# Two durations in a build-time instruction planner set to other values: the issue and the landing of the loads of split rows

## The chip, the core and the metric

The kernel runs on one core of a Trainium2 chip. The metric is the device time of one launch in microseconds (us); each kernel is run several times and the median is compared. Times of single instructions come from one profiled execution.

## What is computed

Two transformer layers over 4 batches of 1024 tokens with 256 features, 16 heads of 16. Cut to what matters, with layer normalisation after each residual sum:

```python
x = norm(x + L0_attn(x))   # rotary, causal softmax within a window of 64 tokens
x = norm(x + L0_ffn(x))    # token shift, sigmoid gate, squared relu
x = norm(x + L1_attn(x))   # linear attention over random features
x = norm(x + L1_ffn(x))    # a whole block: norm, rotary, full causal softmax, then a routed
                           # feed-forward: 8 experts, top 2, capacity 1024 each
```

All of it is float32 at the inputs and outputs.

## The kernel before

There are two stages. The **first stage** holds both attentions, the two small feed-forward and linear-attention parts, and the routing. The **second stage** runs the 8 experts and the last normalisation. The second stage is written in a fixed order and the change doesn't reach it.

The first stage is cut into 32 groups of 4 heads, in this order: 4 windowed groups of batch 0, 4 windowed of batch 1, 4 full of batch 0, 4 windowed of batch 2, 4 full of batch 1, and so on; so groups 0 to 3 are windowed, 8 to 11 full, 20 to 23 windowed. Two groups make a pair, and each pair is prepared together (`prep`): projections (`proj`, L928), rotary products, sums on GpSimd (`add`), transposes back (`turn`, L947), and a split of each float32 row into three bfloat16 parts (`high`, `mid`, `low`) in the tile `b_split`. Twelve **loads** per group (`load`, L760, issued by SyncE, 128 KB each) bring the parts into one of three ring tiles `b_qk`. A group's `max` products (a mask product L955 or L958, then L962) wait for all twelve of its loads. Their row maxima are reduced on VectorE (`reduce`, L1378), turned (`rows`, L968), written back to `b_qk` by a small DMA (`spread`, L767), and then the `exp` products (L975), the exponentials on ScalarE (L1114) and the products with the values (`values`, L989) follow; `out` (L997) turns the sums back.

No engine's order is written by hand. The class `Planner` lists every step with an engine, an assumed cost and what it comes after, and simulates the engines at build time. At each moment an idle engine takes, among the steps that are ready by the plan, the one with the longest chain of assumed costs behind it. A step that follows one on another engine becomes ready after that engine's delay in `LATE`, or, if it follows a DMA, after that kind's entry in `LANDING`. What comes out is a program for each engine, which the hardware then runs in that order with semaphores. SyncE's order is planned in the same way: the loads, the spreads, and the `zeros` (L790), 32 DMAs of 256 KB that clear a DRAM buffer, are all in one queue.

The plan leaves one more mark in the program. Where it sees TensorE idle for more than 1.0 us before a step that takes a PSUM bank, filler products (L808) are put in front of that step, for 0.6 of the planned idle time at 0.064 us each:

```python
for n in range(int(FILLED * plan.idle[x] / FILLER) if plan.idle[x] > LEAST_IDLE else 0):
    pe.matmul(u.psum[:, plan.bank[x], 0:P], u.id16[:, :], u.id16[:, :], start=True, stop=True, ...
```

The names that the prediction uses: `LANDING` in `Planner`, `load` inside `describe` of `Plan`, the pair's last `turn` (L947), a group's first `max` (L955 or L958), the fillers (L808), the `zeros` (L790) and the spreads (L767).

## Time and profile before

| | us |
|---|---|
| median of 3 runs (lowest to highest) | 1862.9 (1861.72 to 1863.72) |
| the profiled execution | 1861.47 |
| its span, first to last instruction | 1859.7 |
| TensorE busy | 1733.4 (93%) |
| VectorE busy | 1016.1 (55%) |
| ScalarE busy | 886.3 (48%) |
| GpSimd busy | 835.7 (45%) |
| mean granted TensorE clock, share of full speed | 0.975 |

In the profile PE is TensorE, PEld its weight loads, DVE VectorE, ACT ScalarE, POOL GpSimd and SPq the DMA queue of SyncE. A row names the source line, the operation and the tiles it writes and reads. Busy time doesn't count waiting for semaphores. The granted clock is the share of TensorE's full speed (2.4 GHz) that it was given.

### The profile page before, as it was taken

Reading aid. Unit: us, or ns where it says so; the run is one execution under the profiler, and the core shown is the slowest. Engines: PE = TensorE matmul, PEld = TensorE weight load, DVE = VectorE, ACT = ScalarE, POOL = GpSimd, SP = SyncE. Lnnn points to the kernel's source line nnn. Section 1 sums busy time; section 2 is a strip of 40 time slices with the busy share of each in tenths; the row PEclk is TensorE's granted clock in tenths of the full one; section 3 lists DMA queues with packets and bytes.
Section 4 is the critical chain, followed back from the end, with each engine's and each line's share of the span. In section 5 each row is a group of like instructions: output and inputs, shape, how many; then the busy total and the mean of one; then the engine's idle time right before and its main releaser. Section 6 shows DMA issues by size and latency. Waiting matters only on the chain. (4 is left out here: it accounts for less than half of the span.)

```text
span 1859.7 us, 34083 instructions
## 1 busy us (share of the span) xinstructions
PE 1733.4 (93%) x11399; PEld 1130.5 (61%) x11399; DVE 1016.1 (55%) x2357; ACT 886.3 (48%) x1877; POOL 835.7 (45%) x1295
## 2 busy tenths in 40 slices
PE   6899998999999899999999999999879999999992
PEld 5666765665476656557765654544647766667771
DVE  4557677868567985857698677885401100011014
ACT  2455463657756365675637467566322222212223
POOL 4674663522368683137868323455432211221223
PEclk9999999999999999999999999999889999999996
DMA  6725337132343313234512214242033233332116
GB/s 211 95 71 68 44 103 131 19 52 92 47 71 75 87 24 47 70 50 69 91 29 36 35 47 70 44 76 71 29 122 85 40 65 83 90 88 62 20 23 192
DMA packets 106055, 131.27 MB, mean 71 GB/s; under 512 B 15882, under 2 KB 77467, under 8 KB 105744
## 3 DMA queue, kind: packets, MB, share of 16 engines
q1 hardware_dynamic: 89488, 117.08, 29.6%
q0 software_dynamic: 14336, 11.41, 4.5%
q8 instruction: 98, 1.61, 0.4%
q14 instruction: 69, 0.57, 0.2%
q10 hardware_dynamic: 2064, 0.61, 0.2%
HBM read 53.96 MB, written 38.01 MB: 49 GB/s over the span
## 5 line engine op out<-in xcount | busy, mean ns | idle before, releaser
L1114 ACT ACTIVATE b_probs<-b_psum 128x512 f32<-128x512 f32 (+3 forms) x896 | 417.8, 546 | 184.3 <-PE b_psum L975 182.6
L1378 DVE TENSOR_REDUCE b_mneg<-b_psum 128x2 f32<-128x384 f32 (+5 forms) x608 | 331.9, 591 | 88.5 <-PE b_psum L962 87.2
L1477 POOL TENSOR_SCALAR_AFFINE_SELECT b_probs<-b_probs 128x512 f32<-128x512 f32 (+1 forms) x400 | 239.3, 610 | 284.7 <-ACT b_probs L1114 273.9
L962 PE MATMUL b_psum<-b_qk 96*128 96x192 bf16 (+4 forms) x1280 | 292.5, 294 | 3.1 <-DVE b_mhalf L1378 1.1
L975 PE MATMUL b_psum<-b_qk 99*128 99x192 bf16 (+5 forms) x1344 | 261.5, 289 | 11.3 <-DMA b_qk<-b_mrow 7.0
L1711 POOL DMA_INDIRECT before_last_norm<-b_ye,b_ids x64 | 99.1, 1549 | 347.6 <-DMA before_last_norm<-b_ye,b_ids 195.2
L1808 ACT ACTIVATE b_hid<-b_psum,b_b 128x512 f32<-128x512 f32 (+1 forms) x136 | 90.0, 662 | 336.1 <-PE b_psum L1751 336.1
L1852 DVE TENSOR_TENSOR b_ye<-b_psum,b_qk 128x512 f32<-128x512 f32 (+1 forms) x33 | 22.3, 675 | 388.5 <-PE b_psum L1759 388.5
L989 PE MATMUL b_psum<-b_probs,b_v 128*32 128x192 f32 (+4 forms) x2688 | 197.6, 414 | 3.8 <-POOL b_probs L1477 3.0
L962 PEld LDWEIGHTS b_psum<-b_qk 96*128 96x128 bf16 x1280 | 122.8, 99 | 93.4 <-issue 24.7
L1378 DVE TENSOR_REDUCE b_mhalf<-b_psum 128x1 f32<-128x512 f32 x256 | 165.0, 680 | 15.0 <-PE b_psum L962 14.3
L975 PEld LDWEIGHTS b_psum<-b_qk 99*128 99x128 bf16 x1344 | 113.3, 98 | 91.5 <-issue 22.7
L1493 POOL TENSOR_TENSOR b_rot<-b_product 128x128 f32<-128x128 f32 x256 | 113.1, 474 | 120.3 <-PE b_psum L947 52.5
L989 PEld LDWEIGHTS b_psum<-b_probs,b_v 128*32 128x32 f32 x2688 | 68.6, 109 | 92.7 <-issue 66.5
L1361 DVE TENSOR_TENSOR b_product<-b_psum,b_cossin 128x512 f32<-128x512 f32 x128 | 87.7, 687 | 56.5 <-PE b_psum L928 50.6
L928 PE MATMUL b_psum<-b_wqkv,b_xt 128*128 128x384 f32 x320 | 116.7, 493 | 0.5 <-ACT b_xt L1020 0.3
L1759 PE MATMUL b_psum<-b_w,b_hid 128*128 128x256 f32 x512 | 111.6, 379 | 0.6 <-ACT b_hid L1808 0.6
L1751 PE MATMUL b_psum<-b_xgt,b_qk 128*128 128x512 f32 x256 | 110.9, 593 | 0.4 <-ACT b_xgt L1798 0.4
L1759 PE MATMUL b_psum<-b_qk,b_hid 128*128 128x256 f32 x512 | 111.2, 379 | 0.0
L1751 PE MATMUL b_psum<-b_xgt,b_w 128*128 128x512 f32 (+1 forms) x288 | 110.9, 545 | 0.0
L1759 PEld LDWEIGHTS b_psum<-b_w,b_hid 128*128 128x128 f32 x512 | 97.0, 190 | 14.0 <-ACT b_hid L1808 1.0
L1759 PEld LDWEIGHTS b_psum<-b_qk,b_hid 128*128 128x128 f32 x512 | 97.0, 190 | 13.0
(227 smaller groups left out, 2772.9 us busy)
## 6 DMA issues: line engine op xcount, KB each, us to landing
b_qk<-b_split SPq DMA_DIRECT2D x372, 128.0 KB, 5.5
slot_rows<-before_last_norm SPq DMA_DIRECT2D x32, 256.0 KB, 3.9
b_qk<-in_W SPq DMA_DIRECT2D x8, 1024.0 KB, 7.5
b_xg<-slot_rows SPq DMA_DIRECT2D x16, 512.0 KB, 9.6
b_w<-in_W SPq DMA_DIRECT2D x8, 1024.0 KB
before_last_norm<-b_early SPq DMA_DIRECT2D x4, 1024.0 KB, 4.4
b_o<-before_last_norm SPq DMA_DIRECT2D x4, 1024.0 KB, 5.5
before_last_norm<-b_o SPq DMA_DIRECT2D x4, 1024.0 KB, 4.5
```

What stands on the lines that cost most here:

```text
L928: ins = pe.matmul(u.psum[:, plan.bank[x], 0:384].rearrange("p (a g y) -> p a g y", a=3, g=2), x_rows[:, c, P * t:P * t + P], (u.wqkv0 if n ...
L962: ins = pe.matmul(out[:, i, :], q[0:KS, h, P * t:P * t + P], q[0:KS, HG + h, a:e], start=not last, stop=True, skip_group_check=True)
L975: ins = pe.matmul(out[:, i, :], q[0:KM, HG + h, P * t:P * t + P], q[0:KM, h, a:e], start=True, stop=True, skip_group_check=True)
L989: ins = pe.matmul(sums_of(g, h2)[32 * h:32 * h + 32, a - BANK * h2:e - BANK * h2], u.v[:, g % 4, t, (HD + 1) * h:(HD + 1) * h + 32], probs ...
L1114: act.activation(probs_of((g, h2, t), a, e)[:, heads[0]:heads[-1] + 1, :], bank, ACT.Exp, scale=SCALE).then_inc(s.exp_done, 1)
L1378: dve.tensor_reduce(out, in_bank(("max",) + x[1:], heads, e - a), AX.X, ALU.max, negate=True).then_inc(s.max_read, 1)
L1477: ins = pool.affine_select(out=block, in_=block, pattern=[[0, HG], [1 if ahead else -1, z - y]], compare_op=ALU.is_ge, fill=none, base=y - ...
L1493: ins = pool.tensor_tensor(out[:, :, :, HALF * y:HALF * y + HALF], straight[:, :, :, HALF * y:HALF * y + HALF], crossed[:, :, :, HALF * (1 ...
L1711: pool.indirect_dma_start(out=x4_dram, out_offset=bass.IndirectOffsetOnAxis(ap=u.ids[:, column:column + 1], axis=0), in_=u.ye[t // 2][:, t ...
L1751: ins = pe.matmul(u.psum[:, k % 4, 0:hi - lo], u.w1[e % 2][:, c, P * n:P * n + P], u.xgt[:, c, lo:hi], start=(c == 0), stop=(c == NC - 1))
L1759: ins = pe.matmul(u.psum[:, bank_of(e, t), D * (t % 2):D * (t % 2) + D], u.hid[:, n, P * t:P * (t + 1)], u.w2[e % 2][:, n, :], start=(n == ...
L1808: act.activation(u.hid[:, n, lo:hi], u.psum[:, k % 4, 0:hi - lo], ACT.Gelu, bias=u.b1[:, NF * e + n:NF * e + n + 1]).then_inc(s.h_done, 1)
```

## The change

Two assumed durations of the loads of split rows are replaced. The time from issue to landing becomes 5.1 in place of 4.5, and the time that SyncE takes for one issue becomes 0.69 in place of 1.05. Only the loads of group 0 keep their own issue cost of 0.55.

```diff
-    LANDING = {"load": 4.5, "spread": 2.2, "source": 4.0, "x3_in": 3.0, "x3_out": 3.0, "x4_out": 3.0, "put": 2.5, "zeros": 6.0, "expert": 8.0}
+    LANDING = {"load": 5.1, "spread": 2.2, "source": 4.0, "x3_in": 3.0, "x3_out": 3.0, "x4_out": 3.0, "put": 2.5, "zeros": 6.0, "expert": 8.0}
...
-                        add(("load", g, a, slot, y), "SP", 0.55 if y is not None else 1.05, (kind, g // 2, q), last)
+                        add(("load", g, a, slot, y), "SP", 0.55 if y is not None else 0.69, (kind, g // 2, q), last)
```

No instruction of the computation is added or removed. The program of each engine is another order of the same steps, and the number of fillers is another: 475 in 26 places before, 348 in 15 places now. The last three places (50, 12 and 22 fillers) are the same in both. Up to the first filler place and in the last 131 rows of TensorE the two orders agree; between, they differ nearly throughout. Three places are shown.

TensorE near the start, after the second half of group 0's `max` products, as one piece of the difference (- before, + now). L808 are the fillers, L968 turns the row maxima of group 0, L928 are the projections of the second pair:

```order
 L955 MATMUL b_psum<-b_mask_q,b_id 128x2x192
 L962 MATMUL b_psum<-b_qk 128x192 x2
-L808 MATMUL b_psum<-b_id 128x128 x32
-L968 MATMUL b_psum<-b_id,b_mparts 128x128 x4
+L808 MATMUL b_psum<-b_id 128x128 x14
 L928 MATMUL b_psum<-b_wqkv,b_xa 128x384 x8
 L947 MATMUL b_psum<-b_id,b_rot 128x128 x4
```

The projections now come ahead of the turn of the maxima, with 18 fillers fewer before them.

TensorE up to the first `max` of group 20, whose first row is L955. The pair's last `turn` is the row L947. Before, that row stands 13 rows above the first one shown, and behind the rows shown come twelve short L975 (128x384, 128x256 and 128x128, four each) and L955:

```order
L997 MATMUL b_psum<-b_id,b_ot_sb 128x128 x4
L989 MATMUL b_psum<-b_probs,b_v 32x256 x4
L989 MATMUL b_psum<-b_probs,b_v 32x128 x4
L975 MATMUL b_psum<-b_qk 128x512 x8
L997 MATMUL b_psum<-b_id,b_ot_sb 128x128 x8
L808 MATMUL b_psum<-b_id 128x128 x12
L722 MATMUL b_psum<-b_id,b_y 128x128 x8
L989 MATMUL b_psum<-b_probs,b_v 32x512 x8
L975 MATMUL b_psum<-b_qk 128x512 x12
L716 MATMUL b_psum<-b_wproj,b_early 128x256 x4
L989 MATMUL b_psum<-b_probs,b_v 32x512 x8
```

Now, from the last `turn` on; behind the rows shown come one more L997 x4, L989 512 x8, the same twelve short L975, and L955:

```order
L947 MATMUL b_psum<-b_id,b_rot 128x128 x4
L975 MATMUL b_psum<-b_qk 128x512 x5
L989 MATMUL b_psum<-b_probs,b_v 32x256 x4
L989 MATMUL b_psum<-b_probs,b_v 32x128 x4
L997 MATMUL b_psum<-b_id,b_ot_sb 128x128 x4
L975 MATMUL b_psum<-b_qk 128x512
L997 MATMUL b_psum<-b_id,b_ot_sb 128x128 x4
L722 MATMUL b_psum<-b_id,b_y 128x128 x4
L997 MATMUL b_psum<-b_id,b_ot_sb 128x128 x4
L989 MATMUL b_psum<-b_probs,b_v 32x512 x8
L975 MATMUL b_psum<-b_qk 128x512 x12
```

The pair's last `turn` has moved nearer to the first `max` that needs its loads, and the fillers and the projection L716 have gone from between them.

SyncE's queue around the loads of groups 8 and 9; L760 are the loads, L790 the zeros, L767 the spreads. Before:

```order
L767 DMA b_qk<-b_mrow 3x4x512
L760 DMA b_qk<-b_split 16x4x1024 x10
L790 DMA slot_rows<-before_last_norm 128x2x256 x7
L760 DMA b_qk<-b_split 16x4x1024
L767 DMA b_qk<-b_mrow 3x4x512
L760 DMA b_qk<-b_split 16x4x1024 x13
```

Now:

```order
L760 DMA b_qk<-b_split 16x4x1024 x4
L767 DMA b_qk<-b_mrow 3x4x512
L760 DMA b_qk<-b_split 16x4x1024 x2
L790 DMA slot_rows<-before_last_norm 128x2x256 x2
L760 DMA b_qk<-b_split 16x4x1024 x4
L790 DMA slot_rows<-before_last_norm 128x2x256 x4
L760 DMA b_qk<-b_split 16x4x1024 x12
```

Group 8's twelve loads now have six zeros and one spread between them, where they had seven zeros and one spread; the last two of them are the first two of the last row. The other groups' loads mostly run through without a spread between them: 12 of the 30 groups from 2 on have one or more now, 20 had before.

## Rows read from the trace of the kernel before

**Rows 1.** Busy time by stretch: start:end, length, then PE, PEld, DVE, ACT, POOL, clock.

```profile
30.00:1290.00 1260.00, 1203.92 (x9166) 765.63 (x9165) 917.38 (x2031) 724.42 (x1599) 668.57 (x1118) 0.99 0.35 65
1290.00:1362.00 72.00, 49.13 (x432) 35.13 (x433) 23.75 (x118) 23.16 (x48) 23.32 (x25) 0.77 0.07 24
```

**Rows 2.** The same view, fillers (L808) alone: length, PE and PEld busy, clock.

```profile
30.00:1290.00 1260.00, 28.68 (x391) 25.84 (x391) 0.99 0.35 65
```

**Rows 3.** Groups of PE: count, then busy us, mean ns, idle before and releasers.

```profile
L955 PE MATMUL b_psum<-b_mask_q,b_id 128*128 128x384 bf16 (+1 forms) x256 | 82.9, 327 | 6.5 <-DMA b_qk<-b_split 4.5 <-DVE b_mneg L1378 1.7
...
L808 PE MATMUL b_psum<-b_id 128*128 128x128 bf16 x475 | 35.6, 237 | 10.4 <-DVE b_mneg L1378 4.5 <-DVE b_mhalf L1378 3.0 <-ACT b_mrow L1138 1.6
```

**Rows 4.** PE in order of time at the start: start, length, line, idle before.

```profile
46.98 1.95 PE L808 MATMUL b_psum<-b_id 128*128 128x128 bf16 x32
50.07 0.40 PE L968 MATMUL b_psum<-b_id,b_mparts 128*128 128x128 bf16 x4 [1.14 <-POOL b_mparts L1426]
```

**Rows 5.** DMA issues of the page: count, KB each, median us to landing.

```profile
b_qk<-b_split SPq DMA_DIRECT2D x372, 128.0 KB, 5.5
...
b_qk<-b_split SPq DMA_DIRECT2D x24, 64.0 KB, 2.6
```

**Rows 6.** SyncE's queue in order of time, loads of groups 8 and 20.

```profile
276.26 6.47 SPq L760 DMA_DIRECT2D b_qk<-b_split  x10
282.78 5.56 SPq L790 DMA_DIRECT2D slot_rows<-before_last_norm  x7
288.81 0.58 SPq L760 DMA_DIRECT2D b_qk<-b_split  x1
...
817.32 1.96 SPq L760 DMA_DIRECT2D b_qk<-b_split  x3
...
820.54 15.41 SPq L760 DMA_DIRECT2D b_qk<-b_split  x21
```

**Rows 7.** Line L760, landing in stretches 270 to 310, 816 to 838, 493 to 515.

```profile
DMA to landing us min/median/max: 5.9/7.8/9.1
...
DMA to landing us min/median/max: 6.8/8.7/10.0
...
DMA to landing us min/median/max: 3.4/4.2/5.7
```

**Rows 8.** PE in order of time, last turn to first max, group 8.

```profile
274.94 0.65 PE L947 MATMUL b_psum<-b_id,b_rot 128*128 128x128 f32 x4
...
288.93 1.17 PE L808 MATMUL b_psum<-b_id 128*128 128x128 bf16 x9
...
291.74 3.69 PE L716 MATMUL b_psum<-b_wout,b_xa 128*128 128x256 f32 x16 [0.73 <-issue]
...
296.79 0.39 PE L958 MATMUL b_psum<-b_causal_q,b_id 128*128 128x512 bf16 x1
```

**Rows 9.** The same view, group 20.

```profile
815.92 0.66 PE L947 MATMUL b_psum<-b_id,b_rot 128*128 128x128 f32 x4
...
822.66 0.86 PE L989 MATMUL b_psum<-b_probs,b_v 128*32 128x256 f32 x16
...
825.19 1.04 PE L997 MATMUL b_psum<-b_id,b_ot_sb 128*128 128x128 f32 x8
...
830.30 3.43 PE L975 MATMUL b_psum<-b_qk 99*128 99x512 bf16 x12
...
835.75 1.92 PE L989 MATMUL b_psum<-b_probs,b_v 128*32 128x512 f32 x16
837.61 1.48 PE L975 MATMUL b_psum<-b_qk 99*128 99x384 bf16 x12
838.93 0.27 PE L955 MATMUL b_psum<-b_mask_q,b_id 128*128 128x256 bf16 x1
```

**Rows 10.** The same view, two filler places of equal count.

```profile
158.93 1.39 PE L808 MATMUL b_psum<-b_id 128*128 128x128 bf16 x22
...
321.45 2.49 PE L808 MATMUL b_psum<-b_id 128*128 128x128 bf16 x22 [2.02 <-DVE b_mhalf L1378]
```

**Rows 11.** Busy time by stretch, columns as in rows 1.

```profile
321.00:324.00 3.00, 2.55 (x23) 2.55 (x24) 2.86 (x10) 0.24 (x2) 0.00 (x0) 0.59 0.00 0
```

## Prediction

> **What bounds the kernel now.** I read the busy time by stretch first. Between 30 and 1290 us, the stretch that the planner orders, TensorE is busy for 1203.9 of 1260.0 us, VectorE for 917.4 and ScalarE for 724.4 [rows 1]. So TensorE sets the time there. What an order can still change is its slack: 1260.0 - 1203.9 = 56.1 us of idle time, and the fillers, 391 of them for 28.7 us [rows 2], together 84.8 us. The products themselves are the same in any order. From 1290 on (49.1 of 72.0 us busy up to 1362 [rows 1]) the last 131 rows of TensorE's order don't change, and behind that comes the expert stage, which the change doesn't touch.
>
> Next I read, in the groups of PE, what TensorE waits for. For the loads it waits 4.5 us in all [rows 3]. That is little: in this order the loads are almost always there before they are asked for. The wait ahead of fillers is 10.4 us, and VectorE ends most of it [rows 3]. So the old, dear price of a load did not show as a wait. It showed in where the plan put other work.
>
> Then I read the loads themselves. Ten issues take 6.47 us, or 0.65 us each [rows 6], so 0.69 is near the trace and 1.05 was 0.40 too dear. From issue to landing the median is 5.5 us [rows 5], so 5.1 is nearer than 4.5 and still short. It isn't one number, though: the stretches have medians of 4.2, 7.8 and 8.7, and single landings up to 10.0 [rows 7]. For a pair's second group the plan now sees the last landing at 24 x 0.69 + 5.1 = 21.7 us after the first issue, where it saw 24 x 1.05 + 4.5 = 29.7; for the first group 13.4 in place of 17.1.
>
> **The change, part by part.**
>
> *Fillers.* In the stretch that changes there were 475 - 84 = 391 and now there are 348 - 84 = 264, that is 127 fewer (the last three places hold 84 in both). One costs 28.68 / 391 = 73 ns [rows 2], so 127 x 0.073 = 9.3 us of TensorE's time leave the program. Fewer fillers mean that the plan has found work for places where it saw TensorE idle. The place near the start shows it: the 32 fillers took 1.95 us, and another 1.14 us were idle before the turn of the maxima [rows 4]; now 18 of them are gone and the projections, which wait for nothing new, stand there. At the first place the plan adds 6 fillers; TensorE waits there for loads in any case (part of the 4.5 us of rows 3), so they cost nothing unless those loads land earlier than before.
>
> *Idle time next to fillers.* Of the 23 places in the stretch 12 are left. If the idle time goes with the places, 10.4 x 11 / 23 = 5.0 us go too. The bounds are 0 (the waits move to where no filler stands) and 10.4 (all of it). I take 5.0, since in the trace the planned idle places were idle in fact: a filler place that runs full and still waits stands in rows 4, one that starts late in rows 10.
>
> *The load waits that come up.* This is what the cheaper price costs. Where a first `max` was planned with time to spare it is now planned tight, and a landing later than 5.1 us makes TensorE wait. I work out the two places with the worst landings.
>
> Group 20: before, the last turn began at 815.92 and the first `max` at 838.93, a gap of 23.0 us [rows 9]. In the new order I add up what stands there, with the rows of the old trace: the turn 0.5, six long L975 as half of 3.43, the short `values` 0.86, five turns (L997 and L722) at 1.04 / 2 each, two `values` at 1.92 each, twelve long L975 3.43, the short L975 1.48 [rows 9], together 14.4 us. The loads need: from the start of the turn to the first issue 817.32 - 815.92 = 1.4, eleven more issues at 0.65 = 7.2, then a landing [rows 6]. With 3.4 that makes 12.0, with the 8.7 of this stretch 17.3, with 10.0 it makes 18.6 [rows 7]. The wait is 0 to 4.2 us; I take 3, close to this stretch's own median.
>
> Group 8: before, the gap was 296.79 - 274.94 = 21.9 us [rows 8]. The output projection L716 (3.69) and its nine fillers (1.17) [rows 8] no longer stand in it, so about 17.0 are left, with the small waits of before in it. The loads now run with six zeros and a spread between them: 276.26 - 274.94 = 1.3 to the first issue, 11 x 0.65 = 7.2, six zeros at 5.56 / 7 = 0.79, a spread of about the same [rows 6], 14.0 in all; then 5.9 to 9.1 for the landing [rows 7]. The wait is 2.9 to 6.1 us; I take 4.5, the middle, since 7.8 is the stretch's median.
>
> At the first groups of four more pairs (4, 12, 24, 28) the order has shortened the same gap, by less; I have no landing row for each. By the stretch with 4.2 us [rows 7] the wait is 0, by the one with 8.7 some 3 us each, 12 in all. I take 1 us for the four, since they are nearest to the quiet stretch: group 12's loads are those at 493 to 515. All load waits together: 3 + 4.5 + 1 = 8.5 us, with bounds of 2.9 and 22.3. A wait here holds all that is queued on TensorE behind it. It holds no spread on SyncE longer, since loads go out in their order either way.
>
> *The spreads.* They are in one queue with the loads and now stand behind longer runs of them. TensorE's order is made from the same plan, so it has other work meanwhile; I cost it at nothing. If that cover were gone, a spread behind two more loads would be 2 x 0.65 = 1.3 us late [rows 6].
>
> The sum: -9.3 - 5.0 + 8.5 = -5.8 us. On the profiled execution (1861.5, span 1859.7) that gives 1855.7; the median of the runs shown is 1.4 above that execution, so the forecast is **1857**. This case's own range is 1848 to 1863: with the load waits at 2.9 the sum is -11.4, or -14 with some idle time more; with 14 us it is nothing.
>
> Here a rule differs from the trace. In rows 5 a load of 128 KB lands after 5.5 us and one of 64 KB after 2.6. The Trainium skill (DMA: Bandwidth & Descriptors, Anatomy of one DMA) fits a DMA that GpSimd issues as about 2.0 us plus the bytes at 436 GB/s; by that a load of 128 KB would take an estimated 2.3 us, the load waits would be nothing, and the sum would be -14.3. The trace doesn't agree: these loads are issued back to back by SyncE, and rows 7 hold landings four times as long.
>
> **The rivals.**
>
> *The loads were hidden anyway.* The change is then only another shuffle: what the fillers free comes back as small waits on VectorE, which is busy for 73% of the stretch [rows 1]. For it speaks that TensorE waited for loads for 4.5 us only [rows 3]; against it, that the places with planned idle time fell by half. The 14.3 us come back in full: 1863, with 1859 to 1867 around it. Chance 0.25.
>
> *The tight loads become the bound* (slower). The place is the first `max` of each pair, the price the upper bounds: 4.2 + 6.1 + 12 = 22.3 us against 14.3, so +8.0 and 1871. From 14.3 us of load waits on there is no gain left, and from 18 on it is measurably slower. For it speaks that two of the three bursts in rows 7 land after 7.8 and 8.7 us while the plan books 5.1. Against it: the burst with 4.2, and that a waiting TensorE lets VectorE and ScalarE catch up. Chance 0.22.
>
> *The clock.* Twenty-two fillers took 1.39 us at one place and 2.49 at another, after a wait of 2.02 us [rows 10], and the granted clock in that stretch was 0.59, a mixture of the two levels of 1.2 and 2.4 GHz [rows 11]. If the places that lose their fillers stand idle in their stead, nothing of the 9.3 us is saved, and 11 drops at 2.49 - 1.39 = 1.1 us are added: +12, or 1875. By the Trainium skill (TensorE: Matmul & The Clock Gate, What's actually happening) the throttled clock is the default and recent activity releases it, which speaks against taking fillers away; in rows 10 and 11 the fillers themselves ran slow after the wait, so here they did not hold the clock up through it. Against this rival: the fillers went because work took their place. Chance 0.05.
>
> *Every load lands early.* If all landed as the small ones did, in 2.6 us [rows 5], no wait would come up: -14.3, or 1849. Rows 7 speak against it. Chance 0.06. By the Trainium skill (DMA: Bandwidth & Descriptors, Anatomy of one DMA) the outcome would be about this one.
>
> That the change does nothing can be left out: the order differs nearly throughout.
>
> **How the numbers follow.** My forecast has 0.42, the others 0.25, 0.22, 0.05 and 0.06. A measurement of this kernel can tell about 0.2%, that is 3.7 us, from no change: below 1859.2 is faster, above 1866.6 slower. Faster: 0.36 of my forecast, 0.05 of the shuffle, 0.06 early landing, 0.47. The same: 0.06 of my forecast, 0.16 of the shuffle, 0.04 of the tight loads, 0.26. Slower: 0.04, 0.18 and 0.05 for the clock, 0.27. The range reaches from 1847, just under early landing, to 1872, just over the price of the tight loads; beyond it lie the clock, and the outer parts of early landing and of the tight loads, less than 0.2 together.
>
> **What would show it.** Right: fillers at 264 and some 19 us between 30 and 1290; in the groups of PE, waits for `b_split` of 5 to 15 us at L955 and L958, the longest at the first `max` of groups 8 and 20; the stretch to the start of the tail shorter by about 6 us; the expert stage as long as before. Wrong: no waits for `b_split` at all (then the landing or my sums of the gaps are wrong), or idle time that has grown on VectorE's results by as much as the fillers lost (the shuffle), or a granted clock under 0.98 in the stretch (the clock).

## The result, and the profile after

| | before | after |
|---|---|---|
| median of 3 runs (lowest to highest), us | 1862.9 (1861.72 to 1863.72) | 1889.58 (1884.91 to 1891.97) |
| ratio to before, with its 95% interval | 1 | 1.014 (1.0108 to 1.0172) |
| span of the profiled execution, us | 1859.7 | 1883.2 |
| mean granted TensorE clock | 0.975 | 0.968 |

The change made the kernel 1.4% slower. The forecast was 1857 with a range up to 1872, so the sign and the range were both missed.

Where the 23.5 us between the two spans lie can be added up on TensorE, since a span is its busy time plus its idle time. From the groups of PE: without the fillers TensorE was busy for 1697.8 us before and 1711.2 after (+13.4), the fillers took 35.6 and 26.7 (-8.9), and the idle time was 126.3 and 145.3 (+19.0).

The first view is the busy time by stretch of the kernel after. Its columns are those of [rows 1], and behind the clock stand the busy share of the 16 DMA engines and the GB/s that they moved, two columns that [rows 1] have as well and that the prediction left unread:

```profile
30.00:1290.00 1260.00, 1186.90 (x8851) 752.08 (x8848) 898.42 (x1996) 709.95 (x1562) 649.73 (x1092) 0.98 0.37 62
```

Against [rows 1] TensorE does 315 matmuls fewer in the same 1260 us, of which some 127 are fillers: it is behind with its products. The expert stage begins with the row L1740 of PE, which stands in order of time before

```profile
1361.09 5.71 PE L1740 MATMUL b_psum<-b_id 128*128 128x128 f32 x28 [14.91 <-PEq L744]
```

and after

```profile
1384.41 5.70 PE L1740 MATMUL b_psum<-b_id 128*128 128x128 f32 x28 [14.91 <-PEq L744]
```

From there to the end it is 498.6 us before and 498.8 after, so the loss lies in the planned stretch.

The groups of PE after, with the columns of [rows 3]:

```profile
L975 PE MATMUL b_psum<-b_qk 99*128 99x192 bf16 (+5 forms) x1344 | 266.3, 291 | 28.9 <-DMA b_qk<-b_mrow 21.6 <-DVE b_mneg L1378 1.8 <-ACT b_probs L1114 1.3
...
L958 PE MATMUL b_psum<-b_causal_q,b_id 128*128 128x128 bf16 (+2 forms) x352 | 88.3, 251 | 8.0 <-DMA b_qk<-b_split 4.3 <-DVE b_mhalf L1378 1.5 <-DVE b_mneg L1378 0.9
L955 PE MATMUL b_psum<-b_mask_q,b_id 128*128 128x384 bf16 (+1 forms) x256 | 83.9, 331 | 10.1 <-ACT b_probs L1114 4.2 <-DMA b_qk<-b_split 3.7 <-DVE b_mneg L1378 2.1
...
L808 PE MATMUL b_psum<-b_id 128*128 128x128 bf16 x348 | 26.7, 244 | 5.0 <-DVE b_mneg L1378 3.3 <-DVE b_mhalf L1378 1.7
```

The idle time ahead of L975, the `exp` products, is 28.9 us. Before, that row read

```profile
L975 PE MATMUL b_psum<-b_qk 99*128 99x192 bf16 (+5 forms) x1344 | 261.5, 289 | 11.3 <-DMA b_qk<-b_mrow 7.0 <-DVE b_mneg L1378 1.5 <-DVE b_kvm_mt L1173 0.6
```

So +17.6 of the +19.0 us of idle time stand at one line, and the releaser is the spread (`b_qk<-b_mrow`): 7.0 before, 21.6 now. The prediction had costed just this at nothing. It had not read this row in the trace of before, where its 11.3 us are more idle time than stand in the rows it did read. Ahead of the first `max` (L955, L958) the idle time grew by 8.6 and next to the fillers it fell by 5.4; the remainder is -1.8.

The waits of PE after, with the total, the times and the longest one:

```profile
PE b_psum L975 <- DMA b_qk<-b_mrow: 21.6, 11, 6.0
...
PE b_psum L958 <- DMA b_qk<-b_split: 4.3, 1, 4.3
```

The longest of the eleven can be followed over three engines. ScalarE, in order of time (start, length): the copy of the maxima ahead of the spread.

```profile
73.05 0.57 ACT L1138 ACTIVATE b_mrow<-b_psum 12x512 bf16<-12x512 bf16 x1
```

SyncE's queue after:

```profile
65.86 9.78 SPq L760 DMA_DIRECT2D b_qk<-b_split  x13
75.69 0.75 SPq L767 DMA_DIRECT2D b_qk<-b_mrow  x1
76.56 7.37 SPq L760 DMA_DIRECT2D b_qk<-b_split  x9
```

And PE in order of time, with the first `max` of groups 8 and 20 as its last two rows:

```profile
75.20 0.97 PE L989 MATMUL b_psum<-b_probs,b_v 128*32 128x64 f32 x24
82.16 2.50 PE L975 MATMUL b_psum<-b_qk 99*128 99x192 bf16 x16 [5.99 <-DMA b_qk<-b_mrow]
...
291.94 0.58 PE L958 MATMUL b_psum<-b_causal_q,b_id 128*128 128x512 bf16 x1 [4.27 <-DMA b_qk<-b_split]
...
846.58 0.37 PE L955 MATMUL b_psum<-b_mask_q,b_id 128*128 128x256 bf16 x1 [2.09 <-ACT b_probs L1114]
```

The copy was done at 73.62. The spread was issued at 75.69, 2.1 us later, because SyncE had the last of thirteen loads to issue first. Its products began at 82.16, 6.5 us after that issue. The plan had booked 2.2 us for that landing. Two delays, then, and the larger one comes after SyncE has let the spread go.

What keeps it is seen in the same stretch of the busy view:

```profile
78.00:82.00 4.00, 0.00 (x0) 0.00 (x0) 0.00 (x0) 0.00 (x0) 0.36 (x1) 0.58 1.06 125
82.00:84.20 2.20, 2.04 (x14) 1.92 (x15) 0.00 (x0) 1.53 (x5) 0.59 (x1) 0.50 1.09 120
```

While TensorE, VectorE and ScalarE all stand still, the DMA engines are busy for all of the time (1.06; the column can exceed 1 a little) and move 125 GB/s. When TensorE starts again its granted clock is 0.50, the lower of the two levels, where it was 1.00 up to 78 us. By the Trainium skill (TensorE: Matmul & The Clock Gate, What's actually happening) recent activity is what releases the throttle; these rows agree, since nothing but the wait lies between. The sixteen products that follow take 2.50 us for it; ten of the same size took 1.10 us at full clock before (at 68.20 us).

The late landing itself isn't new. Before, the spread of the same place was issued at 75.78 us, behind fourteen loads, and its products began 7.9 us later:

```profile
83.67 1.44 PE L975 MATMUL b_psum<-b_qk 99*128 99x192 bf16 x8 [1.70 <-DMA b_qk<-b_mrow]
```

TensorE had other rows to run until 81.97, eighteen fillers among them, and waited for 1.70 us only, though here too its granted clock was 0.50 behind the wait (83.70 to 86.00 us). What the change took away is the work that covered the landing.

A full burst shows the rate. These are 24 loads in one run, first in SyncE's queue, then in the busy view of the kernel after:

```profile
150.29 16.01 SPq L760 DMA_DIRECT2D b_qk<-b_split  x24
```

```profile
150.00:155.00 5.00, 5.00 (x29) 4.46 (x28) 3.80 (x8) 3.70 (x8) 2.34 (x4) 1.00 0.65 109
155.00:160.00 5.00, 3.22 (x29) 2.64 (x28) 3.76 (x5) 3.59 (x7) 1.00 (x1) 1.00 1.06 121
160.00:165.00 5.00, 5.00 (x17) 2.99 (x16) 3.83 (x8) 1.72 (x3) 2.73 (x3) 1.00 1.10 124
165.00:170.00 5.00, 5.00 (x29) 4.34 (x28) 4.44 (x17) 4.78 (x10) 1.77 (x2) 1.00 1.09 118
170.00:175.00 5.00, 5.00 (x36) 4.06 (x35) 4.79 (x16) 2.53 (x5) 4.07 (x3) 1.00 1.11 125
175.00:180.00 5.00, 5.00 (x24) 3.62 (x23) 4.86 (x14) 1.71 (x5) 1.89 (x5) 1.00 0.33 38
```

SyncE has issued all of them by 166.3. The DMA engines work on until about 176.5, some 26 us after the first issue, or 1.1 us a load; 131,072 bytes at the 118 to 125 GB/s of the four full stretches are 1.05 to 1.11 us, and 1.07 at their mean. So a load has two prices: 0.65 us of SyncE [rows 6] and 1.07 us of the DMA engines. In a run each load adds the difference, 0.42 us, to a queue behind SyncE; after twelve it is 5.0 us deep. The answer on line L760 for this stretch says what that does to the landing; it covers the last twelve of the 24 loads, whose landing climbs along the run from 8.0 us for the first of them to 12.5 for the last, 0.41 us a load:

```profile
DMA to landing us min/median/max: 8.0/10.4/12.5
```

The burst of before ran at the same rate; the trace of before has, for one such stretch,

```profile
150.00:155.00 5.00, 5.00 (x22) 3.84 (x21) 4.14 (x14) 2.90 (x7) 2.04 (x2) 1.00 1.07 124
155.00:160.00 5.00, 5.00 (x43) 4.47 (x43) 2.51 (x5) 4.94 (x10) 0.00 (x0) 1.00 1.11 124
```

The row was there to be read, and the old value of 1.05 was close to it. It had been booked as SyncE's time, which it isn't, but it lies close to the time of the resource that limits the loads in a run. Here a rule bears on the price: the Trainium skill (SBUF — State Buffer, Door 1: The DMA port swizzle) says that DMA bandwidth depends on how many of the 16 ports the partitions reach. By its formula the 16 partitions of one load reach 4 ports, an estimate of 4/16 of 435 GB/s, 109 GB/s or 1.2 us a load. The rows of these bursts come near it, 8 to 15% above, at 118 to 125 GB/s; no run here shows that the ports are what sets the rate.

### The profile page after: what moved, and what is told of

Same layout as the page of the kernel before. It is cut to its first block and busy times, and to the rows that moved or that the text cites. A ratio compares the mean times of both kernels' runs of the same rounds, so it can differ in the third digit from the quotient of the medians.

```text
span 1883.2 us, 33834 instructions
## 1 busy us (share of the span) xinstructions
PE 1737.9 (92%) x11272; PEld 1126.5 (60%) x11272; DVE 1015.3 (54%) x2357; ACT 889.9 (47%) x1877; POOL 834.7 (44%) x1295
## 3 DMA queue, kind: packets, MB, share of 16 engines
q1 hardware_dynamic: 89488, 117.08, 30.7%
## 5 line engine op out<-in xcount | busy, mean ns | idle before, releaser
L962 PE MATMUL b_psum<-b_qk 96*128 96x192 bf16 (+4 forms) x1280 | 299.2, 300 | 3.7 <-DVE b_mhalf L1378 1.3
L975 PE MATMUL b_psum<-b_qk 99*128 99x192 bf16 (+5 forms) x1344 | 266.3, 291 | 28.9 <-DMA b_qk<-b_mrow 21.6
L1852 DVE TENSOR_TENSOR b_ye<-b_psum,b_qk 128x512 f32<-128x512 f32 (+1 forms) x33 | 22.3, 675 | 388.5 <-PE b_psum L1759 388.5
L989 PE MATMUL b_psum<-b_probs,b_v 128*32 128x192 f32 (+4 forms) x2688 | 197.6, 416 | 1.9 <-POOL b_probs L1477 1.6
L975 PEld LDWEIGHTS b_psum<-b_qk 99*128 99x128 bf16 x1344 | 113.9, 98 | 116.9 <-issue 42.7
L989 PEld LDWEIGHTS b_psum<-b_probs,b_v 128*32 128x32 f32 x2688 | 69.6, 110 | 91.7 <-issue 66.6
L928 PE MATMUL b_psum<-b_wqkv,b_xt 128*128 128x384 f32 x320 | 117.7, 492 | 1.8 <-DVE b_mneg L1378 1.1
```

The source lines that it names most:

```text
L928: ins = pe.matmul(u.psum[:, plan.bank[x], 0:384].rearrange("p (a g y) -> p a g y", a=3, g=2), x_rows[:, c, P * t:P * t + P], (u.wqkv0 if n ...
L962: ins = pe.matmul(out[:, i, :], q[0:KS, h, P * t:P * t + P], q[0:KS, HG + h, a:e], start=not last, stop=True, skip_group_check=True)
L975: ins = pe.matmul(out[:, i, :], q[0:KM, HG + h, P * t:P * t + P], q[0:KM, h, a:e], start=True, stop=True, skip_group_check=True)
L989: ins = pe.matmul(sums_of(g, h2)[32 * h:32 * h + 32, a - BANK * h2:e - BANK * h2], u.v[:, g % 4, t, (HD + 1) * h:(HD + 1) * h + 32], probs ...
```

## The experiments

After the result six theories stood against each other. **S**: the spreads land some 6 us after their issue, behind loads, and the plan books 2.2. **L**: the loads land later than the 5.1 booked. **N**: any other order from this planner costs about this much, and before was a lucky one. **D**: 1.05 was the DMA engines' time for a load, and a plan with 0.69 promises all that comes behind loads too early. **R**: the price acts through the priority of steps (the longest chain behind them), not through the simulated times. **O**: the new order is bad in itself, whatever the loads do. In what follows "waits" are those of TensorE for the spread and for the loads, in that order, from the groups of PE.

### One half of the change alone

`issue_only` is the kernel before with the new issue price:

```diff
-    add(("load", g, a, slot, y), "SP", 0.55 if y is not None else 1.05, (kind, g // 2, q), last)
+    add(("load", g, a, slot, y), "SP", 0.55 if y is not None else 0.69, (kind, g // 2, q), last)
```

> Only the issue cost changes (1.05 to 0.69); the landing stays 4.5. Theory S (the spreads, 12 KB DMAs in one queue with the loads, land about 6 us after their issue where the plan books 2.7, and loads booked cheaper put them behind longer runs of loads): the slowdown comes with the issue cost, so 1875 to 1895 us and TensorE waits for b_mrow of 15 to 25 us (7.0 before, 21.6 after). Rival L (the landing of the loads sets when the first max products are placed): close to before, 1858 to 1868. Rival N (any new order moves the time by this much, whatever the numbers): no telling, but the waits for b_mrow need not grow.

`landing_only` is the kernel before with the new landing:

```diff
-    LANDING = {"load": 4.5, "spread": 2.2, ...
+    LANDING = {"load": 5.1, "spread": 2.2, ...
```

> Only the landing changes (4.5 to 5.1); the issue cost stays 1.05. Theory S: the plan still leaves as much room between loads and spreads, so 1855 to 1870 us and waits for b_mrow of 5 to 10 us. Rival L: also about 1860, since later landings are the safe side. Rival N: a shift of more than 10 us either way with waits that don't come from b_mrow.

Measured: `issue_only` 1879.16 us, ratio 1.0095 (1.0078 to 1.0112), waits 24.1 and 14.9 us. `landing_only` 1859.29 us, 0.9994 (0.998 to 1.0007), waits 5.8 and 3.9. The issue price alone brings the spread waits up, as its row of L975 shows:

```profile
L975 PE MATMUL b_psum<-b_qk 99*128 99x192 bf16 (+5 forms) x1344 | 267.5, 291 | 28.3 <-DMA b_qk<-b_mrow 24.1 <-DVE b_mneg L1378 1.5 <-ACT b_probs L1114 0.9
```

The landing alone moves the order and costs nothing, which speaks against N: a shuffle by itself need not cost 1%. The price alone gives about two thirds of the loss; why the longer landing, harmless alone, adds the rest on top of it isn't shown.

### The spread's landing, in the plan and on another queue

`spread_booked` is the kernel after, with the spread's landing booked as the trace shows it:

```diff
-    LANDING = {"load": 5.1, "spread": 2.2, ...
+    LANDING = {"load": 5.1, "spread": 5.5, ...
```

> The changed kernel with the landing of the spreads booked at 5.5 in place of 2.2, which with its issue of 0.5 is the 6 us that the waits for b_mrow show. Theory S: the plan puts other work ahead of the first exp products, the waits for b_mrow fall from 21.6 to under 8 us, and with the clock that they cost the time falls by 15 to 25 us, to 1865 to 1875. Rival L: the waits for b_split (8.0 us) and the time stay as after, 1880 to 1895. Rival N: waits for b_mrow gone, but the time anywhere between 1855 and 1895.

`after_spread_act` is the kernel after in its own order, with the spreads issued by ScalarE on its own queue, right behind the copy:

```diff
-    sp.wait_ge(s.rows_read, n + 1)
-    sp.dma_start(u.qk[g % RING][KS:KS + 3, 0:HG, ...], u.mrow[n % 2][0:3 * HG, :]
-                 ).then_inc(rows_sent[n % 2], 16)
+    pass
...
+    act.wait_ge(s.rows_read, n + 1)
+    act.dma_start(u.qk[g % RING][KS:KS + 3, 0:HG, ...], u.mrow[n % 2][0:3 * HG, :]
+                  ).then_inc(rows_sent[n % 2], 16)
```

> The changed kernel's order on TensorE, VectorE and GpSimd, but the spreads are issued by ScalarE on its own queue right after the copy they send, so no load stands in front of them. It costs ScalarE 64 issues and 64 waits for its own copy. Theory S: the waits for b_mrow fall from 21.6 to under 8 us; time 1865 to 1880, unless ScalarE's added 64 x 1.4 = 90 us show elsewhere as waits for b_probs. If the slow landing is not the queue but the data of the loads on the same DMA engines, the waits stay at 15 us or more and the time at 1885 or above.

Measured: `spread_booked` 1877.86 us, 1.0099 (1.0079 to 1.0119). Its spread waits fell to 2.7 us, as S expected, but the load waits rose to 13.7, TensorE's own work is still 14.4 us longer than before, and the time is 3 us above the range of S. `after_spread_act` 1914.05 us, 1.029 (1.027 to 1.0309): the waits are 27.5 and 12.9, not smaller. The place of the 5.99 us wait reads, in order of time (the lines of the products are shifted by two in this kernel, L973 is L975, and L1138 is the issue of the spread), first on ScalarE:

```profile
73.02 0.74 ACTq L1138 DMA_DIRECT2D b_qk<-b_mrow  x1
```

and on PE:

```profile
78.70 2.11 PE L973 MATMUL b_psum<-b_qk 99*128 99x192 bf16 x16 [3.17 <-DMA b_qk<-b_mrow]
```

The spread left at once after the copy and still took 5.7 us to its products. The two loads that SyncE issued next to it, at 72.7 and 73.4 us, landed no sooner:

```profile
DMA to landing us min/median/max: 6.1/6.3/6.5
```

So standing behind loads in SyncE's queue isn't what makes it late; by these rows it comes through about when the loads of its own time do, behind the data of the earlier ones. By the Trainium skill (DMA: Bandwidth & Descriptors, Queues, rings and completion order) a DMA engine takes turns between queues packet by packet, by which a small DMA on a queue of its own should pass the loads. This run doesn't show that benefit: 5.7 us against 6.5. The run tells of the delay alone: ScalarE now spends 0.72 us (median) on each of the 64 issues as well, so its time isn't comparable; the 1.4 us of the expectation stand in no run. S is right about the delay, but booking it mends only part of the time.

### The price as a dose

The kernel before, with other issue prices in place of 1.05:

```diff
-    add(("load", g, a, slot, y), "SP", 0.55 if y is not None else 1.05, (kind, g // 2, q), last)
+    add(("load", g, a, slot, y), "SP", 0.55 if y is not None else 0.88, (kind, g // 2, q), last)
```

> The kernel before with an issue cost of 0.88, half way between 1.05 and 0.69; landing 4.5. Theory D: what 1.05 stood for is not SyncE's time but that of the DMA engines, which move one load of 128 KB at 120 to 125 GB/s in 1.05 to 1.09 us, while SyncE issues one every 0.65; so each load booked below 1.05 promises its data too early by the difference, and the last of 24 by 24 times it. Then 0.88 costs part of what 0.69 costs (0.95%): 0.2 to 0.8% over before, with waits for b_mrow and b_split together between the 11.5 us of before and the 39 us of the run with the issue cost alone. Rival N (any new order costs this, whatever the numbers): no order between the values; as likely over 1% as under 0.

```diff
+    add(("load", g, a, slot, y), "SP", 0.55 if y is not None else 1.25, (kind, g // 2, q), last)
```

> The kernel before with an issue cost of 1.25, above what the DMA engines need; landing 4.5. Theory D: too dear is the safe side: waits for b_mrow and b_split together at or under the 11.5 us of before, time within 0.5% of before. Rival N: a slowdown by some 1% here as well, as with any new order.

```diff
+    add(("load", g, a, slot, y), "SP", 0.55 if y is not None else 1.50, (kind, g // 2, q), last)
```

> The kernel before with an issue cost of 1.50 (1.25 gave a ratio of 0.996). Theory R and theory D both: pairs are prepared still earlier, waits for b_mrow and b_split stay at or under 8 us; but loads booked at 1.50 make the plan itself idle (565 fillers against 490 at 1.25, that is 5.5 us more), so no further gain: 1852 to 1866 us. If the trend went on by itself it would be about 1847.

| issue price booked | median us | ratio to before (95%) | both waits, us |
|---|---|---|---|
| 0.69 (`issue_only`) | 1879.16 | 1.0095 (1.0078 to 1.0112) | 39.0 |
| 0.88 | 1868.51 | 1.0047 (1.0031 to 1.0063) | 20.6 |
| 1.05 (before) | | 1 | 11.5 |
| 1.25 | 1854.1 | 0.9961 (0.9946 to 0.9976) | 7.7 |
| 1.50 | 1867.79 | 1.0034 (1.0022 to 1.0047) | 8.0 |

The waits fall with the price up to 1.25 and stay there. The time falls with them up to 1.25; at 1.50 it is up again, 2 us above its range. Its profile has 3.3 us more of fillers than before and 4.1 us more of TensorE's own work, at the same idle time, so this rise isn't one of waits. The order by size up to 1.25 is what D says and N doesn't. The kernel with 1.25 is faster than both kernels of this case.

### A later landing instead

`landing_88` is the kernel after, with the landing of a load as late as the deep bursts of [rows 7]:

```diff
-    LANDING = {"load": 5.1, "spread": 2.2, ...
+    LANDING = {"load": 8.8, "spread": 2.2, ...
```

> The changed kernel (issue 0.69) with the loads' landing booked at 8.8 in place of 5.1, so that twelve loads come out as before: 12 x 0.69 + 8.8 = 12 x 1.05 + 4.5. Theory D: it mends a pair's first group but not its second (24 x 0.36 = 8.6 us early against 4.3 us of longer landing) nor the spreads behind the loads: faster than the changed kernel, waits for b_split under 5 us, waits for b_mrow still 10 us or more, 1863 to 1878 us. Rival L (only the constant landing was too short): 1855 to 1865.

Measured: 1901.78 us, 1.0214 (1.0197 to 1.023), far above the ranges of both D and L. The load waits did fall, to 3.2 us, but the spread waits rose to 47.4 (16 times, longest 8.6). One fixed landing, however late, doesn't stand in for the queue: the spreads behind the loads are still promised in 2.2 us. That this is why they rose was only argued. L, as a cure, falls.

### Priority or simulated time

The price enters the planner twice: as the time for which it books SyncE, and in the length of the chain by which it chooses among ready steps. `rank_069` keeps the simulated times of before and puts the change's numbers into the chain alone:

```diff
-    urgent[x] = st.cost + max([urgent[y] + (... else self.LANDING[x[0]]
+    urgent[x] = (0.69 if x[0] == "load" and x[-1] is None else st.cost) + max([urgent[y] + (... else 5.1 if x[0] == "load" else self.LANDING[x[0]]
```

> The kernel before, but where the planner ranks ready steps by the chain of costs behind them, a load counts as 0.69 with a landing of 5.1; the simulated times stay 1.05 and 4.5. Theory R (the issue cost acts through the rank: 24 loads in a chain at 0.36 less make the whole preparation of a pair 8.6 us less urgent, so it is done later and its loads are asked for sooner after they start): close to the run with the issue cost alone, 1870 to 1885 us, waits for b_mrow and b_split together over 20 us. Theory D (the simulated time of the loads is what counts, for 1.05 is what the DMA engines need): close to before, 1855 to 1867, waits under 15 us.

`rank_105` is its mirror: the simulated times of after, and the old 1.05 and 4.5 in the chain.

```diff
-    urgent[x] = st.cost + max([urgent[y] + (... else self.LANDING[x[0]]
+    urgent[x] = (1.05 if x[0] == "load" and x[-1] is None else st.cost) + max([urgent[y] + (... else 4.5 if x[0] == "load" else self.LANDING[x[0]]
```

> The reverse: the changed kernel's simulated times (0.69 and 5.1), but the rank counts a load as 1.05 with a landing of 4.5. Theory R: close to before, 1857 to 1868 us, waits for b_mrow and b_split together under 15 us. Theory D: as slow as the changed kernel, 1875 to 1895 us, waits for b_mrow of 20 us or more, since spreads are still booked as if no loads were queued on the DMA engines ahead of them.

Measured: `rank_069` 1862.32 us, 0.9999 (0.9987 to 1.001), waits 6.2 and 6.1; `rank_105` 1878.04 us, 1.0084 (1.0068 to 1.01), waits 26.7 and 3.6. The slow order goes with the simulated times, so R falls as the account of the whole. It is mostly what the plan believes of when things arrive that costs the time; the step from 1.0084 to the 1.014 of after, where the chain has the new numbers too, stays unexplained.

### Booking both prices

If D is the whole story, a plan that knows both resources should be at least as good as before. `drain_model` books SyncE for 0.65, and beside it a queue of the DMA engines with 1.07 per load, so that what is issued behind a run of loads lands later by what is still queued; a load with nothing queued ahead is booked to land after 3.4 us:

```diff
-    LANDING = {"load": 5.1, "spread": 2.2, ...
+    LANDING = {"load": 3.4, "spread": 2.2, ...
+    DRAIN = {"load": 1.07, "spread": 0.1, "source": 4.0, ... "zeros": 0.9, "expert": 10.0}
...
-    ready = max([done[y] + (... else self.LANDING[y[0]] if y[0] in self.LANDING
+    ready = max([done[y] + (... else self.LANDING[y[0]] + behind.get(y, 0.0) if y[0] in self.LANDING
...
+    if x[0] in self.DRAIN:
+        drain = self.DRAIN[x[0]] * (0.5 if x[0] == "load" and x[-1] is not None else 1.0)
+        behind[x] = max(drained - end, 0.0)
+        drained = max(drained, end) + drain
...
-    add(("load", g, a, slot, y), "SP", 0.55 if y is not None else 0.69, (kind, g // 2, q), last)
+    add(("load", g, a, slot, y), "SP", 0.55 if y is not None else 0.65, (kind, g // 2, q), last)
```

> The changed kernel's plan with both resources booked: SyncE for 0.65 us per load and, beside it, the DMA engines for 1.07 us per load (0.9 per zeros DMA, 0.1 per spread); a load lands 3.4 us and a spread 2.2 us after its issue plus what is queued ahead of it on the DMA engines. Theory D: waits for b_mrow and b_split together under 8 us, time at or below the kernel before, 1848 to 1863 us. Rival N: the time anywhere, 1850 to 1890, whatever the waits.

`drain_rank_125` is the same with a load counted as 1.25 and 4.5 in the chain:

```diff
-    urgent[x] = st.cost + max([urgent[y] + (... else self.LANDING[x[0]]
+    urgent[x] = (1.25 if x[0] == "load" and x[-1] is None else st.cost) + max([urgent[y] + (... else 4.5 if x[0] == "load" else self.LANDING[x[0]]
```

> The plan with both resources booked (SyncE 0.65 per load, DMA engines 1.07), and the rank counting a load as 1.25 with a landing of 4.5. It was 0.73% slower than before with the rank counting 0.65, though its waits for loads and spreads were small. Theory R: the early preparation comes back, and with right times besides it is at or under the run with 1.25 alone, 1845 to 1860 us. If the rank doesn't matter: 1870 to 1880 again.

Measured: `drain_model` 1875.79 us, 1.0073 (1.0059 to 1.0087); `drain_rank_125` 1872.61, 1.0056 (1.0041 to 1.007). Both missed the time that D forecast, although the spread waits are all but gone:

```profile
L975 PE MATMUL b_psum<-b_qk 99*128 99x192 bf16 (+5 forms) x1344 | 259.7, 288 | 10.1 <-DVE b_mneg L1378 2.3 <-ACT b_probs L1114 1.8 <-DVE b_kvm_mt L1173 1.5
```

That is the row of L975 in `drain_model`; the releaser `b_mrow` isn't among the first three any more (1.4 us); the load waits are 7.8, so the two together are just above the 8 expected. In `drain_rank_125` the waits are 0.2 and 6.6, the idle time is 0.2 us above that of before, and yet TensorE's own work takes 11.8 us longer at a granted clock of 0.971. So a plan that foresees the queue removes the spread waits, but it isn't a better plan here: that the wrong price makes these waits is borne out, that a right one makes the kernel fast is not. What makes its order 0.6 to 0.7% slow stays open.

### Half the data in the same order

The last pair tests the cause itself, without moving a single instruction. From group 3 on each load moves 2 of its 4 heads, 64 KB in place of 128; the scores of the other two heads are then computed from what the ring tile holds from earlier groups, so part of the computation is on other data.

```diff
-    sp.dma_start(u.qk[g % RING][HD * slot:HD * slot + HD, HG * a:HG * a + HG, cols],
-                 u.split[HG * HD * (g % 2):HG * HD * (g % 2 + 1), a, part, cols]
+    n = HG // 2 if g >= RING else HG
+    sp.dma_start(u.qk[g % RING][HD * slot:HD * slot + HD, HG * a:HG * a + n, cols],
+                 u.split[HG * HD * (g % 2):HG * HD * (g % 2) + n * HD, a, part, cols]
```

In the order of after:

> The changed kernel, every engine's order as it is, but from group 3 on each load moves 2 of its 4 heads (64 KB in place of 128 KB), so the other two heads work on rows left from an earlier group. Theory D (the DMA engines need 1.07 us per load where the plan books 0.69, and the spreads and the first max products wait behind that queue): a load needs about 0.54 us, less than its issue, so the queue never builds up; waits for b_mrow and b_split together fall from 29.6 to 12 us or less, and the time by 12 to 25 us, to 1863 to 1876. Theory O (the order itself is bad: work that is late on VectorE and ScalarE): the waits move elsewhere, time 1880 or above.

and, with the same edit, in the order of before:

> The control: the kernel before, its order as it is, with the same halved loads from group 3 on. Theory D: this order books 1.05 per load and hardly waits for loads or spreads (11.5 us), so it gains little: 1853 to 1863 us. Theory O: no more and no less than the changed kernel gains. If it gains as much as the changed kernel does, the gap of 25 us isn't the queue's.

Measured: `after_half_loads` 1861.58 us, 1.0004 (0.999 to 1.0018); `before_half_loads` 1856.86 us, 0.998 (0.9965 to 0.9995). Halving the data takes 25 us off the order of after by the ratios (28 by the medians) and 4 to 6 off that of before, and the gap between the two orders shrinks from 26.7 us to 4.7. The rows of `after_half_loads`, from SyncE's queue, the busy view of the same burst, the groups of PE and the waits:

```profile
149.92 16.21 SPq L760 DMA_DIRECT2D b_qk<-b_split  x24
```

```profile
155.00:160.00 5.00, 3.23 (x28) 2.52 (x27) 4.12 (x6) 3.23 (x7) 0.64 (x1) 1.00 0.38 92
160.00:165.00 5.00, 5.00 (x18) 3.12 (x17) 3.84 (x8) 2.02 (x4) 3.10 (x3) 1.00 0.41 99
```

```profile
L975 PE MATMUL b_psum<-b_qk 99*128 99x192 bf16 (+5 forms) x1344 | 266.4, 291 | 13.5 <-DMA b_qk<-b_mrow 8.4 <-ACT b_probs L1114 1.2 <-DVE b_mneg L1378 0.6
```

```profile
PE b_psum L975 <- DMA b_qk<-b_mrow: 8.4, 2, 5.3
```

SyncE issues the 24 loads in the same 16 us, so its price is unchanged. The DMA engines are busy for 0.38 and 0.41 of the time where they had 1.06 and 1.10, so no queue builds up. How soon the halved loads land this trace doesn't tell. That of `before_half_loads` tells it for two thirds of its loads, and the answer on L760 there has a median of 2.2 us (5.5 before):

```profile
DMA to landing us min/median/max: 2.2/2.2/7.9
```

The spread waits fall from 21.6 to 8.4 us. Of these 8.4 one wait makes 5.3. It is the place of the 5.99 above:

```profile
82.93 2.50 PE L975 MATMUL b_psum<-b_qk 99*128 99x192 bf16 x16 [5.32 <-DMA b_qk<-b_mrow]
```

Twelve of the thirteen loads ahead of that spread are group 2's, and these were left at 128 KB. Everywhere else the spread waits fell from 15.6 to 3.1 us, and these 3.1 are one wait, at the last spread of the stage:

```profile
1297.61 0.81 PE L975 MATMUL b_psum<-b_qk 99*128 99x512 bf16 x3 [3.09 <-DMA b_qk<-b_mrow]
```

Before (3.26) and after (3.08) have it too; no loads of split rows are near it, but two weight loads of 1 MB (L1616 and L1617) are issued ahead of that spread, and the edit leaves them as they are. The nine other waits of after, 12.5 us, are gone. Where the bytes stayed, the wait stayed; where they were halved, it went. With this, D is shown for the waits on the spreads, and O falls as the main cause: with halved loads the two orders are 4.7 us apart.

Two limits remain. The price isn't simply one per byte: a halved load keeps the engines busy for about a quarter of what a whole one does, not half (an estimate from the shares and GB/s of the two bursts). It also has 32 DMA packets fewer (the page's queue q1 goes from 89488 to 78352 for 348 halved loads), so bytes and packets aren't told apart. And the two profiled spans differ by 18.7 us only, since that of after is the fastest of three runs and that of `after_half_loads` the slowest of ten; 12.7 of them are idle time. How the rest of the gain comes about is open.

The load waits didn't follow: 8.9 us against 8.0, so that both kinds together are 17.3 where 12 or less was expected. Group 8's is still there (4.47 us). Its last loads stand behind four zeros of 256 KB, which the edit leaves as they are; whether the zeros make it wasn't tried.

## Why the prediction was wrong

- **Fillers, -9.3: right.** 348 are left; their time fell by 8.9 us.
- **Idle time next to fillers, -5.0: right.** It fell by 5.4.
- **Load waits, +8.5: right in size by luck in part.** The idle time of L955 and L958 rose by 8.6. Group 8 was forecast at 4.5 and waited 4.27. Group 20, forecast at 3, waited 2.09, but the profile puts that on ScalarE's exponentials, as it does a second wait of L955 (4.2 us together); of the 8.6 only 3.5 us are put on loads.
- **The spreads, "I cost it at nothing": this step failed.** The waits for them rose by 14.6 us, from 7.0 to 21.6, and the idle time of L975 by 17.6. The bound given, 1.3 us for two more loads, was wrong by the resource: it took SyncE's 0.65 us per load and left out the data. A spread behind a run of twelve loads has 5.0 us of queue ahead of it (12 x 0.42), and one measured 6.5 us from issue to products.
- **"TensorE's order is made from the same plan, so it has other work meanwhile": wrong.** The plan that orders TensorE is the one that believed the spread would land in 2.2 us, so it placed the products at that time. Before, the price of 1.05 had left other rows in such a place, and a landing of 7.9 us cost 1.70 of wait; at 0.69 one of 6.5 us cost 5.99. An error in the plan is no cover for itself.
- **No term for slower work.** TensorE's own work took 13.4 us longer in the profiled executions, and the prediction took it as the same in any order. The clock after the 5.99 us wait was 0.50, but so it was at that place before. That the spread waits make these 13.4 us isn't shown: `landing_only`, where no waits rose, has 8.3 us more than before at a granted clock of 0.971; runs of the kernel before, all in one order, went from 1852.05 us at 0.979 to 1867.28 at 0.967; and with half the data 9.6 of the 13.4 stayed (1711.2 to 1707.4).
- **The rivals.** "The tight loads become the bound" had the sign and the idea of tighter planning, but at another line and for another DMA, and its 22.3 us of waits are less than the 19.0 of idle time and the 13.4 of slower work together. Its 1871 was 19 us short of the median. The clock rival's sign, a granted clock under 0.98 in the stretch, didn't come: it was 0.98.
- **The reading behind it.** "0.69 is near the trace and 1.05 was 0.40 too dear" is true of SyncE's issue [rows 6]. The landings in [rows 7], 4.2 in one stretch and 8.7 in another, were read as scatter. They go by how deep the queue is: 0.41 us more from load to load in the burst of 24, at a DMA share of over 1.

Still open: why the plans that book the spreads well (`spread_booked`, `drain_model`, `drain_rank_125`) stay 0.6 to 1.0% above before, and how much of that is the clock. They show that an order from this planner can cost that much with few spread waits, so N isn't excluded as a part; for the order of after the halved loads leave 4.7 us to it.

## What to carry to other kernels

A DMA in a planner has two prices, the issuing engine's time per instruction (here 0.65 us) and the DMA engines' time for its data (here 1.07 us for 128 KB in a run of such loads), and what stands behind a run pays the larger one. Before a constant is replaced by a measured one, ask which resource the old value stood for: read the DMA share over a whole burst, not the spacing of the issues or one median landing. Small DMAs on which the bounding engine waits are the ones to follow first, since they are short in bytes and late by what is ahead of them.

## What the runs showed that was not expected

- Loads of 128 KB into 16 partitions keep all 16 DMA engines busy (share 1.06 to 1.11) at only 118 to 125 GB/s, while the zeros go faster: the stretch from 282 to 288 us of the kernel after, with zeros in it, moved 279 GB/s at a share of 0.99. Loads of 64 KB in the same burst took a share of 0.38 to 0.41 at 92 to 99 GB/s.
- A 12 KB DMA on another engine's queue came hardly sooner through a burst than one in the same queue: 5.7 us against 6.5.
- An assumed price that is a little too dear was the better side to err on: 1.25 gave 0.9961 (0.9946 to 0.9976) of before with its 1.05, the fastest median here. It is one plan; whether the price or the particular order did it isn't shown.
